# Attention maxima from three of six bf16 products on two halves of the array's rows, with PSUM evictions moved to ScalarE and numerators copied out early

## The chip, the cores and the metric

The kernel runs on one core of one Trainium2 chip. The metric is the device time of one execution in microseconds (us), the median over runs. Engines are named as in the profile: PE (TensorE matmul), PEld (its weight loads), DVE (VectorE), ACT (ScalarE), POOL (GpSimd), SP (SyncE, which here only issues DMAs).

## The reference, cut to what matters

The program is one layer of three parts on an input of 2 x 1024 x 512: a differential attention with a low-pass filter over time, a second attention-like block, and a mixture of experts. The change lies in the first part:

```
q, k = rope(x @ Wq), rope(x @ Wk)            # 16 heads, each with two streams w of D = 16
s[w] = q[w] @ k[w].T * D**-0.5, causal mask  # T = 1024 queries and keys
a[w] = softmax(s[w]);  o[w] = a[w] @ v       # v has 2*D = 32 columns per head
y    = lowpass(o[0] - lambda * o[1])         # rfft, times a Gaussian, irfft along T
y    = y * rsqrt(mean(y*y over 32) + eps) * w_rms * (1 - LAMBDA_INIT);  out = y @ Wout
```

## The kernel before, in words

The function `attention` handles 8 groups g (2 batches x 4 groups of 4 heads), each with two streams: 16 "sets" n = 2g + w. In float32 the scores would need slow matmuls, so q and k are each cut into three bf16 pieces (16 rows each) and six products of pieces are summed by stacking them along the contraction: `qst` and `kst` hold 6 x 16 = 96 rows for each of the 4 heads, and two more rows (96, 97) that carry the softmax shift as two bf16 pieces against ones.

For each set the kernel does two passes over the scores. The **rows** pass (L703 to 718) computes scores with queries on the partitions, 96 rows deep, and DVE takes minus their maximum along the keys (L839, `maxima`). The maxima of a half of the queries are cut into two bf16 pieces on DVE (`shift_pieces`, L820 to 823), turned by PE into a row (`shifts`, L696), copied by DVE (L830), and brought by two DMAs on SP's queue (`shift_in`, L586 to 590) into rows 96 and 97 of `qst`. The **probs** pass (L720 to 733) computes the scores again with keys on the partitions, 98 rows deep, so that they come out with the shift subtracted; ACT takes their exp into `prob` (L951). Each four heads of one block of keys then make one **values** step (L735 to 749): float32 matmuls of the probabilities with v into `acc` and with ones into `den`, four heads side by side on 32 output columns each ("128*32" in the profile). When a half of the queries is done, ACT makes 1/den (`norm`, L939 and L941) and DVE multiplies and adds into `oT` (`output`, L847, or L851 and L854). The next half's first values step waits for `s_den` and `s_acc`.

All of PE's score units share five PSUM banks (RING = 5): a unit waits in `slot_free` until the unit five before it was read. One PSUM bank, `misc`, serves everything else in turn: the projections of group g + 2 (`project`, in sets with odd n), and in sets with even n the chain of group g - 1: `turn` (transposes), `low` (the filter, six parts), `square` (mean of squares). DVE reads `misc` in all of these (L786, L800, L801, L807, L812, L830), and POOL applies the rotation and cuts the pieces (`rotate`, L966 to 975, seven operations, then a DMA of the pieces) and does the squares and the last scaling (L988, L994 to 998).

The order of the work is a list made by `schedule`: units of set n's probs are merged evenly with those of set n + 1's rows (48 and 38, so 86 to a set), and every other step is put behind a unit by a fixed count. Every engine walks that one list in order. SP's queue has an order of its own (L626 to 645): in each set it issues `stack(n + 2)` (12 DMAs), `shift_in(n + 1, 0)`, for even n `store(g - 1)`, which waits for POOL's last scaling, in the last but one set also `weights_ahead` (11 DMAs of the next part's weights), and then `shift_in(n + 1, 1)`.

## Time and profile before

| | us |
|---|---|
| median of 3 runs (lowest to highest) | 1603.81 (1602.01 to 1616.31) |
| the profiled execution, its own time | 1599.38 |
| its span, first to last instruction | 1597.8 |
| PE matmul busy / DVE / ACT / POOL busy in the span | 1326.1 / 946.8 / 511.7 / 569.5 |
| mean granted clock of TensorE | 0.925 of 2.4 GHz |

The program runs three stages: normalisation up to 71 us, attention from 74 to about 1093 us, the rest behind that. Busy time of PE overlaps between neighbouring matmuls, since their ends are modelled, so spacings from start to start are what one costs in a stream.

### The profile page before, as it was taken

Reading aid. Unit: us, or ns where it says so; the run is one execution under the profiler, and the core shown is the slowest. Engines: PE = TensorE matmul, PEld = TensorE weight load, DVE = VectorE, ACT = ScalarE, POOL = GpSimd, SP = SyncE. Lnnn points to the kernel's source line nnn. Section 1 sums busy time; section 2 is a strip of 40 time slices with the busy share of each in tenths; the row PEclk is TensorE's granted clock in tenths of the full one; section 3 lists DMA queues with packets and bytes.
Section 4 is the critical chain, followed back from the end, with each engine's and each line's share of the span. In section 5 each row is a group of like instructions: output and inputs, shape, how many; then the busy total and the mean of one; then the engine's idle time right before and its main releaser. Section 6 shows DMA issues by size and latency. Waiting matters only on the chain. (4 is left out here: it accounts for less than half of the span.)

```text
span 1597.8 us, 23263 instructions
## 1 busy us (share of the span) xinstructions
PE 1326.1 (83%) x8077; PEld 683.6 (43%) x8092; DVE 946.8 (59%) x1774; ACT 511.7 (32%) x1149; POOL 569.5 (36%) x655
## 2 busy tenths in 40 slices
PE   6867989989989989989989999875688978875985
PEld 5623334434433434433433434332566655552542
DVE  6558666556565566565565566317577655542886
ACT  2200533533433433433433454533112111110121
POOL 4425133333333333333333300200277666663211
PEclk9988999999989999989999999987799998997998
DMA  4345332232231231221331230302222221012331
GB/s 147 120 118 90 74 61 60 42 60 61 41 61 53 49 57 57 48 43 54 53 55 51 43 55 2 120 1 94 78 68 67 67 66 62 36 47 79 123 102 40
DMA packets 70713, 103.92 MB, mean 65 GB/s; under 512 B 10064, under 2 KB 36048, under 8 KB 70608
## 3 DMA queue, kind: packets, MB, share of 16 engines
q1 hardware_dynamic: 58832, 69.00, 19.7%
q0 software_dynamic: 7168, 25.17, 4.5%
q10 hardware_dynamic: 4608, 8.39, 1.4%
q8 instruction: 61, 1.00, 0.3%
q14 instruction: 44, 0.36, 0.1%
HBM read 68.72 MB, written 33.82 MB: 64 GB/s over the span
## 5 line engine op out<-in xcount | busy, mean ns | idle before, releaser
L839 DVE TENSOR_REDUCE nm<-score 128x1 f32<-128x512 f32 (+3 forms) x608 | 379.0, 658 | 287.1 <-PE score L716 156.9
L951 ACT ACTIVATE prob<-score 128x512 f32<-128x512 f32 (+3 forms) x768 | 347.7, 490 | 530.4 <-PE score L731 340.5
L727 PE MATMUL score<-qst,kst 98*128 98x512 bf16 (+3 forms) x768 | 250.5, 342 | 9.1 <-DVE nm L839 4.0
L711 PE MATMUL score<-kst,qst 96*128 96x512 bf16 (+3 forms) x768 | 232.2, 341 | 10.4 <-DMA kst<-piece_scratch 5.4
L746 PE MATMUL acc<-prob,vg 128*32 128x512 f32 (+3 forms) x1536 | 173.9, 526 | 41.9 <-DVE second L851 20.9
L746 PE MATMUL den<-prob,ones 128*32 128x512 f32 (+3 forms) x1536 | 169.8, 514 | 0.0
L660 PE MATMUL misc<-xnT,wg 128*128 128x512 f32 x256 | 137.8, 638 | 21.8 <-DVE raw L786 14.8
L966 POOL TENSOR_TENSOR rot<-raw,cos 128x1024 f32<-128x1024 f32 x14 | 32.8, 2341 | 328.4 <-DVE swapped L792 328.4
L727 PEld LDWEIGHTS score<-qst,kst 98*128 98x128 bf16 x768 | 75.9, 99 | 143.8 <-issue 88.8
L711 PEld LDWEIGHTS score<-kst,qst 96*128 96x128 bf16 x768 | 71.9, 102 | 119.6 <-issue 70.3
L731 PE MATMUL score<-mask_t,identb 128*128 128x128 bf16 x512 | 111.2, 223 | 0.0
L988 POOL TENSOR_TENSOR sq<-y 128x512 f32<-128x512 f32 x14 | 14.5, 1036 | 230.4 <-DVE y L807 161.9
L716 PE MATMUL score<-mask_s,identb 128*128 128x128 bf16 (+2 forms) x352 | 89.2, 254 | 0.0
L746 PEld LDWEIGHTS den<-prob,ones 128*32 128x32 f32 x1536 | 53.5, 116 | 80.9 <-issue 75.1
L1291 PE MATMUL m_b<-m_winh,m_hTh 128*128 128x512 f32 x192 | 85.8, 447 | 2.5 <-DVE m_hTl L1423 2.5
L1291 PE MATMUL m_b<-m_winh,m_hTl 128*128 128x512 f32 x192 | 77.7, 404 | 0.0
L1291 PE MATMUL m_b<-m_winl,m_hTh 128*128 128x512 f32 x192 | 77.0, 401 | 0.0
L746 PEld LDWEIGHTS acc<-prob,vg 128*32 128x32 f32 x1536 | 31.9, 110 | 100.2 <-ACT prob L951 79.6
L660 PEld LDWEIGHTS misc<-xnT,wg 128*128 128x128 f32 x256 | 45.2, 202 | 53.5 <-issue 40.4
L1678 PE MATMUL l_z<-xnT,l_qT 128*128 128x512 f32 x128 | 59.3, 609 | 7.9 <-DMA l_res<-res_scratch 7.9
L731 PEld LDWEIGHTS score<-mask_t,identb 128*128 128x128 bf16 x512 | 51.0, 100 | 29.1 <-issue 16.1
L786 DVE TENSOR_SCALAR raw<-misc 128x512 f32<-128x512 f32 x32 | 22.1, 692 | 67.5 <-PE misc L660 67.4
(227 smaller groups left out, 2140.3 us busy)
## 6 DMA issues: line engine op xcount, KB each, us to landing
piece_scratch<-pieces POOLq DMA_DIRECT2D x16, 768.0 KB, 4.7
qst<-piece_scratch SPq DMA_DIRECT2D x96, 128.0 KB, 5.5
kst<-piece_scratch SPq DMA_DIRECT2D x96, 128.0 KB, 7.5
x1in<-in_query SPq DMA_DIRECT2D x16, 256.0 KB, 2.7
v_scratch<-v ACTq DMA_DIRECT2D x16, 256.0 KB, 2.0
vg<-v_scratch SPq DMA_DIRECT2D x8, 512.0 KB, 6.3
att_scratch<-y SPq DMA_DIRECT2D x8, 512.0 KB, 2.6
m_aT<-att_scratch SPq DMA_DIRECT2D x16, 256.0 KB, 2.9
```

Of the source, the lines that this page charges most:

```text
L660: mm = nc.tensor.matmul(misc[:], wg[:, g % 2, c, w], xnT[:, c, base:base + HALF], start=(c == 0), stop=(c == KC - 1))
L711: mm = nc.tensor.matmul(bank[:, x], qst[0:PROD, n % 4, first + x, i * P:(i + 1) * P], kst[0:PROD, n % 4, first + x, c0:c0 + width], start= ...
L716: mm = nc.tensor.matmul(bank[:, :, width - P:width], identb[:], mask, start=False, stop=True, skip_group_check=True)
L727: mm = nc.tensor.matmul(bank[:, t0:HALF], kst[0:ROWS, n % 4, head, j * P:(j + 1) * P], qst[0:ROWS, n % 4, head, h * HALF + t0:(h + 1) * HA ...
L731: mm = nc.tensor.matmul(bank[:, t0:t0 + P], identb[:], mask_t[:], start=False, stop=True, skip_group_check=True)
L746: mm = nc.tensor.matmul(bank[x, t0:HALF], ones[:] if total else vg[:, n // 2 % 2, j, x], prob[:, (n * NPU + v * GH + head) % NPROB, t0:HAL ...
L786: nc.vector.tensor_scalar(raw[:, half(h)], misc[:], (1.0, float(D) ** -0.5)[w], None, ALU.mult)\
L839: nc.vector.tensor_reduce(dst[:, first:first + heads].rearrange("p (a o) -> p a o", o=1), score[k % RING][:, 0:heads * width].rearrange("p ...
L951: nc.scalar.activation(prob[:, p % NPROB, t0:HALF], score[k % RING][:, t0:HALF], ACT.Exp)\
L966: nc.gpsimd.tensor_tensor(rot[:], raw[:], cos[:], ALU.mult).then_inc(s_cosm, 1)
L1291: mm = mmul(b[:], x[:, c * P:(c + 1) * P], y[:, c, col:col + E], start=(c == 0 and n == 0), stop=(c == KC - 1 and n == 2))
L1678: mm = nc.tensor.matmul(z[t.c % 2][:], qT[:, t.slot, c], rhs, start=(c == 0), stop=(c == KC - 1))
```

## The change

The stacked rows of even and odd heads get different layouts. Even heads have their bands at partitions 0, 16, ... 80 and the shift at 96 and 97, as before; odd heads have them at 64, 80, 96, 16, 32, 48, the shift at 0 and 1, and zeros in rows 2 to 15. The order of pieces is such that the first three bands hold the products 0x0, 1x0 and 0x1. The rows pass now uses these 48 rows alone: partitions 0 to 47 for an even head, 64 to 111 for an odd one. A rows unit is of heads of one parity, units come in pairs (even, odd) whose matmuls alternate and write two banks; there are 40 units to a set where there were 38. The probs pass uses all six products as before (98 rows for even heads, 112 for odd). The list is now merged in pairs (24 + 20 to a set) and all distances are counted in pairs. The steps that share `misc` are kept three pairs apart. ACT instead of DVE copies out `misc` for projections, turns and the filter; DVE keeps the swap, the squares and the shift row. At the end of a half ACT copies `acc` into `accs` in SBUF, on which PE's next values step now waits, and DVE multiplies and adds from that copy. `stack` issues 24 DMAs of half the size, the shift is read back by two DMAs, and POOL sets constants by four memsets, behind the first pieces instead of ahead of them.

```diff
-PROD = 6 * D
-ROWS = PROD + 2
+BANDS = ((0, 16, 32, 48, 64, 80), (64, 80, 96, 16, 32, 48))
+PIECE = ((0, 1, 0, 2, 1, 0), (0, 0, 1, 0, 1, 2))
+COARSE = (slice(0, 3 * D), slice(64, 64 + 3 * D))
+SHIFT = (slice(6 * D, 6 * D + 2), slice(0, 2))
+FULL = (slice(0, 6 * D + 2), slice(0, 64 + 3 * D))
 def rows_units():
     units = []
     for i in range(TB):
         for c0 in range(0, (i + 1) * P, HALF):
             width = min(HALF, (i + 1) * P - c0)
-            n = max(1, HALF // width) if width != 384 else 1
-            units += [(i, c0, width, h, n) for h in range(0, GH, n)]
+            n = 2 if width <= HALF // 2 else 1
+            for first in range(0, 2, n):
+                for odd in range(2):
+                    units.append((i, c0, width, [2 * x + odd for x in range(first, first + n)]))
...
-VALUES_LATER, NORM_LATER, OUT_LATER, SUMS_LATER = 4, 3, 6, 5
+VALUES_LATER, NORM_LATER, OUT_LATER, SUMS_LATER, MISC_FREE = 3, 1, 4, 6, 3
...
+    pairs += [("rows", 0, u) for u in range(0, NRU, 2)]
...
+        mine = [("probs", n, m) for m in range(0, NPU, 2)]
+        ahead = [("rows", n + 1, u) for u in range(0, NRU, 2)] if n + 1 < SETS else []
+        pairs += merge(mine, ahead)
...
+        for h, last in enumerate((at["rows", n, FIRST_HALF - 2], at["rows", n, NRU - 2])):
+            put(last + 1, ("sums", n, h))
+            use(last + SUMS_LATER, ("shift", n, h))
...
-            k = at["probs", n, v * GH + GH - 1] + VALUES_LATER
+            k = at["probs", n, v * GH + GH - 2] + VALUES_LATER
...
-        if n % 2 == 0 and g > 0 or n == SETS:
-            for k, name in zip((14, 17, 27, 41, 46, 54), ("turn", "turn", "low", "low", "square", "square")):
-                use(s + k, (name, g - 1, int(k in (17, 41, 54))))
-            put(s + 50, ("root", g - 1, 0))
-            put(s + 58, ("root", g - 1, 1))
+        s = start[n]
+        if n % 2 == 0 and g > 0:
+            for k, name in zip((8, 10, 17, 23, 27, 30), ("turn", "turn", "low", "low", "square", "square")):
+                use(s + k, (name, g - 1, int(k in (10, 23, 30))))
         if n % 2 and g + 2 < B * G:
-            for k, w, h in ((14, 0, 0), (22, 0, 1), (56, 1, 0), (66, 1, 1)):
+            for k, w, h in ((8, 0, 0), (15, 0, 1), (29, 1, 0), (35, 1, 1)):
                 use(s + k, ("proj", g + 2, w, h))
+    free = 0
+    for first, _, name in sorted(wanted):
+        k = max(first, free)
+        last = PARTS.get(name[0], 1) - 1
+        for part in range(last):
+            put(k + part, ("part", name, part))
+        put(k + last, ("use", name, last))
+        if name[0] == "square":
+            put(k + 2, ("root", *name[1:]))
+        free = k + last + MISC_FREE
...
+                    for odd in range(2):
+                        for r, piece in zip(BANDS[odd], PIECE[w]):
+                            src = piece_scr[g % 2, w, piece].rearrange("(b p w d) t -> w p d b t", p=2, w=2, d=D)
+                            sp.dma_start(parity((qst, kst)[w][r:r + D], odd)[:, slot], src[n % 2, odd])\
+                                .then_inc(s_stack[slot], 16)
...
-                sp.dma_start(qst[PROD:ROWS, n % 4, :, half(h)], shift_scr[n % 2, h]).then_inc(s_shdma[h], 16)
+                for odd in range(2):
+                    sp.dma_start(parity(qst[SHIFT[odd]], odd)[:, n % 4, :, half(h)],
+                                 shift_scr[n % 2, h].rearrange("s (b p) t -> p s b t", p=2)[odd])\
+                        .then_inc(s_shdma[h], 16)
...
+                banks = []
+                for odd in range(2):
+                    slot_free(k + odd)
+                    heads = RU[u + odd][3]
+                    banks.append(score[(k + odd) % RING][:, 0:len(heads) * width]
+                                 .rearrange("p (a s) -> p a s", a=len(heads)))
+                diag = c0 + width == (i + 1) * P
+                for x in range(len(heads)):
+                    for odd in range(2):
+                        c, head = COARSE[odd], RU[u + odd][3][x]
+                        mm = nc.tensor.matmul(banks[odd][:, x], qst[c, n % 4, head, i * P:(i + 1) * P],
+                                              kst[c, n % 4, head, c0:c0 + width], start=(x == 0),
+                                              stop=(x == len(heads) - 1), skip_group_check=True)
+                        if x == len(heads) - 1 and not diag:
+                            mm.then_inc(s_unit, 1)
+                if diag:
+                    mask = mask_s[:].rearrange("p (o s) -> p o s", o=1).broadcast_to([P, len(heads), P])
+                    for odd in range(2):
+                        nc.tensor.matmul(banks[odd][:, :, width - P:width], identb[:], mask, start=False, stop=True,
+                                         skip_group_check=True).then_inc(s_unit, 1)
...
-                    pe.wait_ge(s_acc, 2 * n + h)
+                    pe.wait_ge(s_accs, 2 * n + h)
...
+            def swap(g, w):
+                r = 2 * g + w
+                dve.wait_ge(s_mread, order["proj", g, w, 1])
...
                 if n % 2 == 0:
-                    nc.vector.tensor_tensor(oT[:, half(h)], acc[:], rden[:, q % 2], ALU.mult).then_inc(s_acc, 1)
+                    if g > 0:
+                        dve.wait_ge(s_misc, order["turn", g - 1, h])
+                    nc.vector.tensor_tensor(oT[:, half(h)], accs[:, q % 2], rden[:, q % 2], ALU.mult)\
+                        .then_inc(s_mul, 1)
                 else:
-                    if n > 1 or h:
-                        dve.wait_ge(s_oT, 2 * g + h)
-                    nc.vector.scalar_tensor_tensor(second[:], acc[:], nlam[:], rden[:, q % 2], ALU.mult, ALU.mult)\
-                        .then_inc(s_acc, 1)
-                    dve.wait_ge(s_acc, q + 1)
-                    nc.vector.tensor_tensor(oT[:, half(h)], oT[:, half(h)], second[:], ALU.add).then_inc(s_oT, 1)
+                    nc.vector.scalar_tensor_tensor(accs[:, q % 2], accs[:, q % 2], nlam[:], rden[:, q % 2],
+                                                   ALU.mult, ALU.mult).then_inc(s_mul, 1)
+                    dve.wait_ge(s_mul, q + 1)
+                    nc.vector.tensor_tensor(oT[:, half(h)], oT[:, half(h)], accs[:, q % 2], ALU.add).then_inc(s_oT, 1)
...
+            def project(g, w, h):
+                number, r = order["proj", g, w, h], 2 * g + w
+                act.wait_ge(s_misc, number)
+                if r >= 1:
+                    act.wait_ge(s_cosm, r)
+                nc.scalar.mul(raw[:, half(h)], misc[:], (1.0, float(D) ** -0.5)[w]).then_inc(s_mread, 1)
+            def turned(g, h):
+                act.wait_ge(s_misc, order["turn", g, h])
+                src = misc[:].rearrange("p (j c) -> p j c", j=4)
+                nc.scalar.copy(onat[:, 4 * h:4 * h + 4], src).then_inc(s_nat, 1)
+                nc.scalar.copy(onb[:, 4 * h:4 * h + 4], src).then_inc(s_nat, 1)
+                act.wait_ge(s_nat, 4 * g + 2 * h + 2)
+                act.sem_inc(s_mread, 1)
+            def filtered(g, h):
+                act.wait_ge(s_misc, order["low", g, h])
+                if g >= 1:
+                    act.wait_ge(s_attdma, 16 * g)
+                nc.scalar.copy(y[:, half(h)], misc[:]).then_inc(s_mread, 1)
...
-                if q >= 2:
-                    act.wait_ge(s_acc, q - 1)
+                if n % 2:
+                    act.wait_ge(s_mul, q - 1)
+                elif n > 0:
+                    act.wait_ge(s_oT, n - 1 + h)
                 nc.scalar.activation(rden[:, q % 2], den[:], ACT.Ln).then_inc(s_den, 1)
+                nc.scalar.copy(accs[:, q % 2], acc[:]).then_inc(s_accs, 1)
                 act.wait_ge(s_den, q + 1)
+                act.wait_ge(s_accs, q + 1)
                 nc.scalar.activation(rden[:, q % 2], rden[:, q % 2], ACT.Exp, scale=-1.0).then_inc(s_rden, 1)
...
-            nc.gpsimd.memset(ones[:], 1.0).then_inc(s_ones, 1)
-            pool.wait_ge(s_ones, 1)
-            nc.gpsimd.memset(kst[PROD:P], 1.0).then_inc(s_ones, 1)
-            pool.wait_ge(s_ones, 2)
             for w in range(2):
                 pool.wait_ge(s_rot, 6 * (w + 1))
                 pieces_out(0, w)
+            nc.gpsimd.memset(ones[:], 1.0).then_inc(s_ones, 1)
+            pool.wait_ge(s_ones, 1)
+            nc.gpsimd.memset(parity(kst[SHIFT[0]], 0), 1.0).then_inc(s_ones, 1)
+            pool.wait_ge(s_ones, 2)
+            nc.gpsimd.memset(parity(qst[0:D], 1), 0.0).then_inc(s_ones, 1)
+            pool.wait_ge(s_ones, 3)
+            nc.gpsimd.memset(parity(kst[0:D], 1), 0.0).then_inc(s_ones, 1)
+            pool.wait_ge(s_ones, 4)
+            nc.gpsimd.memset(parity(kst[SHIFT[1]], 1), 1.0).then_inc(s_ones, 1)
+            pool.wait_ge(s_ones, 5)
             pool.wait_ge(s_const, 16 * 12)
```

## Rows read from the trace of the kernel before

**Rows 1.** Busy time by engine, attention and one group of two sets (columns: stretch, length, busy and count of PE, PEld, DVE, ACT, POOL, then clock, DMA share, GB/s).

```profile
150.00:1060.00 910.00, 813.24 (x6062) 352.36 (x6080) 527.76 (x840) 395.03 (x858) 275.89 (x188) 0.95 0.26 53
461.80:582.30 120.50, 107.65 (x782) 47.04 (x784) 72.85 (x113) 50.27 (x108) 41.22 (x29) 0.94 0.26 54
464.00:470.90 6.90, 4.90 (x31) 2.21 (x32) 4.81 (x7) 2.10 (x4) 6.68 (x4) 0.51 0.01 4
```

**Rows 2.** What PE waited for in the same group (us in total, times, longest).

```profile
PE misc L696 <- DVE shp L823: 5.7, 2, 3.9
PE acc L746 <- DVE second L851: 2.5, 2, 1.4
```

**Rows 3.** PE in order of time, 501.1 to 502.8 us (start, duration in us).

```profile
501.23 0.22 PE L731 MATMUL score<-mask_t,identb 128*128 128x128 bf16 x1
501.38 0.64 PE L746 MATMUL acc<-prob,vg 128*32 128x256 f32 x8
501.83 0.61 PE L746 MATMUL den<-prob,ones 128*32 128x256 f32 x8
502.38 0.23 PE L727 MATMUL score<-qst,kst 98*128 98x128 bf16 x1
502.45 0.22 PE L731 MATMUL score<-mask_t,identb 128*128 128x128 bf16 x1
502.51 0.38 PE L711 MATMUL score<-kst,qst 96*128 96x512 bf16 x1
502.73 0.22 PE L716 MATMUL score<-mask_s,identb 128*128 128x128 bf16 x1
```

**Rows 4.** Groups of instructions by line and shape (count, busy us, mean ns, idle before).

```profile
L839 DVE TENSOR_REDUCE nm<-score 128x1 f32<-128x512 f32 x384 | 251.2, 686 | 162.3 <-PE score L711 121.5 <-PE score L716 35.0 <-DVE y L807 0.2
L345 ACT COPY v<-n_vp 128x512 f32<-128x512 f32 x16 | 9.4, 588 | 27.2 <-PE n_vp L325 27.2
```

**Rows 5.** DVE, POOL and PE in order of time, 461 to 466.1 us.

```profile
461.19 2.34 POOL L966 TENSOR_TENSOR rot<-raw,cos 128x1024 f32<-128x1024 f32 x1 [27.29 <-DVE swapped L792]
...
463.49 2.34 POOL L967 TENSOR_TENSOR swapped<-swapped,sin 128x1024 f32<-128x1024 f32 x1
463.59 2.26 DVE L823 TENSOR_TENSOR shp<-nm,shp 128x16 bf16<-128x16 f32 x1
...
466.00 0.37 PE L696 MATMUL misc<-identb,shp 128*8 128x128 bf16 x2 [3.87 <-DVE shp L823]
```

**Rows 6.** DVE and POOL in order of time, 472 to 473.8 us.

```profile
472.05 0.74 DVE L851 SCALAR_TENSOR_TENSOR second<-acc,nlam,rden 128x512 f32<-128x512 f32 x1
472.73 2.13 POOL L975 TENSOR_TENSOR pieces<-rot,pieces 128x1024 bf16<-128x1024 f32 x1
472.83 2.58 DVE L854 TENSOR_TENSOR oT<-oT,second 128x512 f32<-128x512 f32 x1
```

**Rows 7.** The start of attention in order of time.

```profile
74.45 13.75 POOL L1003 MEMSET kst<- 32x16384 bf16 x1
...
98.01 0.69 DVE L786 TENSOR_SCALAR raw<-misc 128x512 f32<-128x512 f32 x1
...
98.84 5.38 PE L660 MATMUL misc<-xnT,wg 128*128 128x512 f32 x8 [6.10 <-DVE raw L786]
...
118.26 2.65 SPq L584 DMA_DIRECT2D kst<-piece_scratch  x6
```

**Rows 8.** POOL's scaling of one group in order of time, first and last of ten operations.

```profile
664.37 1.04 POOL L994 TENSOR_TENSOR newton<-rs 128x512 f32<-128x512 f32 x1 [5.26 <-ACT rs L932]
...
674.88 1.27 POOL L998 TENSOR_TENSOR y<-y,newton 128x512 f32<-128x512 f32 x1
```

**Rows 9.** SP's queue in order of time, 1016 to 1033 us.

```profile
1016.10 0.38 SPq L594 DMA_DIRECT2D att_scratch<-y  x1
...
1025.73 1.89 SPq L588 DMA_DIRECT2D shift_scratch<-shrow  x1
...
1032.35 0.61 SPq L590 DMA_DIRECT2D qst<-shift_scratch  x1
```

**Rows 10.** PE at 1034.55 us, in order of time.

```profile
1034.55 1.89 PE L727 MATMUL score<-qst,kst 98*128 98x512 bf16 x4 [3.40 <-DMA qst<-shift_scratch]
```

More of the change, by code:

```diff
@@ L413, in schedule @@
 def schedule():
-    units, start = [], []
-    units += [("rows", 0, u) for u in range(NRU)]
+    pairs, start = [], []
+    pairs += [("rows", 0, u) for u in range(0, NRU, 2)]
     for n in range(SETS):
-        start.append(len(units))
-        mine = [("probs", n, m) for m in range(NPU)]
-        ahead = [("rows", n + 1, u) for u in range(NRU)] if n + 1 < SETS else []
-        units += merge(mine, ahead)
-    start.append(len(units))
-    at = {u: k for k, u in enumerate(units)}
+        start.append(len(pairs))
+        mine = [("probs", n, m) for m in range(0, NPU, 2)]
+        ahead = [("rows", n + 1, u) for u in range(0, NRU, 2)] if n + 1 < SETS else []
+        pairs += merge(mine, ahead)
+    start.append(len(pairs))
+    at = {u: k for k, u in enumerate(pairs)}
     behind = {}
@@ L427, in put, with use @@
         behind.setdefault(k, []).append(event)
-    def use(k, name, spread=1):
-        last = PARTS.get(name[0], 1) - 1
-        for part in range(last):
-            put(k - (last - part) * spread, ("part", name, part))
-        put(k, ("use", name, last))
+    wanted = []
+    def use(k, name):
+        wanted.append((k - PARTS.get(name[0], 1) + 1, len(wanted), name))
     before = [("use", ("proj", 0, w, h), KC - 1) for w in range(2) for h in range(2)]
@@ L518, in attention @@
         rden = sb("rden", [P, 2, HALF])
-        second = sb("second", [P, HALF])
+        accs = sb("accs", [P, 2, HALF])
         oT = sb("oT", [P, T])
@@ L705, in rows @@
             def rows(n, u):
-                i, c0, width, first, heads = RU[u]
                 k = place["rows", n, u]
-                slot_free(k)
-                bank = score[k % RING][:, 0:heads * width].rearrange("p (a s) -> p a s", a=heads)
-                for x in range(heads):
-                    mm = nc.tensor.matmul(bank[:, x], qst[0:PROD, n % 4, first + x, i * P:(i + 1) * P],
-                                          kst[0:PROD, n % 4, first + x, c0:c0 + width], start=(x == 0),
-                                          stop=(x == heads - 1), skip_group_check=True)
@@ L755, in _ @@
                             pe.wait_ge(s_const, 16 * 12)
[L756 removed]
+                        pe.wait_ge(s_stack[x % 4], 384 * (x // 4 + 1))
                     rows(x, u)
@@ L834, in maxima @@
             def maxima(n, u):
-                i, c0, width, first, heads = RU[u]
+                i, c0, width, heads = RU[u]
                 k = place["rows", n, u]
@@ L880, in _ @@
                         nc.vector.tensor_reduce(lam_e[:], lam_p[:], AX.X, ALU.add).then_inc(s_lam, 1)
+                        begun = 1
+                    maxima(x, u)
+                    maxima(x, u + 1)
+                elif kind == "sums":
+                    shift_pieces(x, u)
+                elif kind == "out":
+                    if (x, u) == (0, 0):
                         dve.wait_ge(s_lam, 4)
@@ L956, in _ @@
                     root(x, u)
-            for h in range(2):
-                root(NG - 1, h)
+                elif kind == "use":
+                    if x[0] == "proj":
+                        project(*x[1:])
+                    elif x[0] == "turn":
+                        turned(*x[1:])
+                    elif x[0] == "low":
+                        filtered(*x[1:])
+            g = NG - 1
+            for h in range(2):
+                turned(g, h)
+            for h in range(2):
+                filtered(g, h)
+            for h in range(2):
+                root(g, h)
         @block.gpsimd
```

145 lines of the change are left out of this document (57 added, 88 removed).

## The prediction

> **What bounds the kernel now.** I read the busy table over stretches first, because the share of the whole span mixes three stages. In attention (150 to 1060 us) PE has matmuls in 813 of 910 us; DVE is busy 58%, ACT 43%, POOL 30% [rows 1]. The stage repeats with a period of two sets, one group: 461.8 to 582.3 is one, 120.5 us, and there are 7.5 of them with two kinds of work merged (15 sets). In it PE idles 12.9 us (120.5 less 107.65), and its granted clock is 0.94. The 6% missing are stretches at the lower level of 1.2 GHz, as 464.0 to 470.9 at 0.51, and they start while PE stands: they cost 0.06 x 120.5 = 7.2 us. That leaves 120.5 - 12.9 - 7.2 = 100.4 us of PE work at full clock.
>
> The waits of PE in this group then say who holds it up: DVE's shift pieces 5.7 and `second` 2.5 [rows 2]; nearly all the rest are DVE too. Why is DVE late when it idles 40% of the time? In order of time L823, a subtraction of 16 numbers, takes 2.26 us while POOL's rotation is in L967, and PE gets its pieces 3.87 us late [rows 5]. At 472.8 L854 (oT + second, both in SBUF) takes 2.58 us beside POOL's L975, but L851, which reads `acc` from PSUM, takes its 0.74 although POOL starts L975 inside it [rows 6]. So a DVE operation with two inputs in SBUF waits until the POOL operation under way ends; one that reads a score or `acc` from PSUM doesn't.
>
> **Part 1, half of the rows matmuls beside the other half.** A set has 18,432 columns of rows matmuls, a group 36,864, or 72 times 512. One of 512 takes 0.22 us from start to start [rows 3]: 15.8 us. If even and odd run side by side, 7.9 go. Taking 48 instead of 96 rows gains nothing by itself: what is paid is columns.
>
> But PE now changes the shape of its array. The trace has this for columns: from the mask (0.06 us for 128 columns, 502.45 to 502.51) to `acc` takes 0.15, so 0.09 extra; `acc` to `den` is 0.45, `den` to the next probs 0.55, so 0.10 extra [rows 3]. One change is 0.095 us. I counted changes along the list of events: 56 in a group before (values and shift rows, in and out), 121 after (36 + 5 into the two halves and 35 + 4 out of them, the rest as before, with some values steps straight beside a rows pair). 65 x 0.095 = 6.2 us come back. No row shows a change of row shape. Its bounds are nothing (6.2 us less) and 0.19, twice the column one (6.2 more, if the second half's weights must also be loaded in the open). I take 0.095, the only change that the trace shows. Sum of part 1: -1.7 us a group. That the two halves overlap at all no row shows either; the four column strips of a values step do: four heads of `acc`, each of 256 columns in float32, take 0.45 us together [rows 3]. I take full overlap; the bound is none, +7.9.
>
> The Trainium skill (TensorEngine Tiling (Array Packing), Key Properties) says that a change of tiling mode "drains the TensorE", and that different tiles run in parallel. The 0.095 us above agree for columns; whether it holds for rows, no run here shows yet. By that page alone the part would be near nothing, as I have it.
>
> DVE has 40 maxima operations in place of 38 with the same elements; two more of 256 columns are well under 2 x 0.69 us [rows 4], beside PE work. The mask matmuls stay (4,096 columns a set).
>
> **Part 2, evictions on ACT, `acc` copied early.** ACT gets 4 projections, 4 turn copies, 2 filter copies and 4 copies of `acc` in a group, 14 x 0.59 = 8.3 us [rows 4]; it goes from 50.3 to 58.6 of about 116 us, beside other work. DVE loses 10 x 0.69. `second` (2.5 us of PE's waiting) goes as a wait; next late is ACT: at a set's end the next values step comes only three probs pairs and a rows pair later, and ln and copy (0.59 each by the copy's row) stand behind two exps. I put 0.5 us a group there, the rest under the stalls of DVE.
>
> **Part 3, POOL against DVE, which speaks against the change.** `output` now reads `accs` and `rden`, two inputs in SBUF, where it read PSUM: the operation that was immune in [rows 6] is so no more. And the steps moved against POOL. A rotation takes 13.7 us (461.19 to 474.86) [rows 5, 6]. I laid the events out with the durations above; times are from a set's start:
> - Odd set, first rotation: before, it began at `sums(n + 1, 0)`, which is why L823 was late. Now the sums are at pair 14, ahead of the projection (pair 18): that wait goes. But `out(n, 0)` at pair 21 falls into the first two POOL operations. It has 1.0 and up to 2.3 us to wait; DVE comes back 3 to 3.5 us late, and five banks cover about one rows pair. PE stands 4.4 us.
> - Even set, second rotation: its projection ends at pair 36 of 44, so POOL works from 3 us ahead of the set to 10 us into it. `sums(n, 1)` waits 2.3 us, `out` 1 to 2: PE stands 3.1 us, about as before.
> - Start of an odd set: POOL's scaling takes 11.8 us [rows 8]. `root(g - 1, 1)` stood behind unit 58 of 86 (67% of the set), now behind pair 39 of 44 (89%), so the scaling reaches 7 us into the next set and delays its sums: 1.6 us.
> - A rows pair needs two banks at once. Between values steps DVE takes 2 x 0.69 for a pair and PE 1.0 for a rows and a probs pair (three times 0.22, 0.19 for the changes, masks): about 0.25 us at 12 of 24 values steps, 3 us.
>
> Together 12.1 + 0.5 = 12.6 us against 12.9. The clock follows long stalls; with one of 4.4 and one of 3.1 in place of more and closer ones I take 5 us for 7.2. Bounds of stalls and clock together: 6 us (DVE is idle often enough that only the 4.4 us remain) and 29 (each collision meets the full 2.3 us).
>
> The skill's page SBUF — State Buffer, Who interferes with whom, has it that a DVE instruction with two SBUF inputs contends with a GpSimd instruction that reads SBUF. The trace agrees in L854 (2.58 us).
>
> A group: -1.7 - 0.3 - 2.2 = -4.2; times 7.5: **-32 us**.
>
> **Part 4, start and end.** In the first group DVE's copy of `misc` stood behind the whole rotation, until 98.01, and PE idled 6.10 us for it [rows 7]. ACT can copy inside that rotation. Then the copy, the next matmuls and their copy (0.69 + 5.38 + 0.69) are done before DVE is free, and its second rotation starts 6.8 us sooner. The rows wait for six more DMA issues of `kst` at 2.65 / 6 = 0.44 us each [rows 7], 2.6: **about -4.5 us** (bounds 0 and -7). The memsets move behind the first pieces and take about twice 13.75 us [rows 7], since each still covers half the columns; POOL's rotation of group 1 moves to about 136 us, with a set to spare. At no cost: DVE is the bound of the first rows pass (38 x 0.69 = 26 us of maxima) and PE's wait there is hidden.
>
> At the end there is a loss. `store(6)` on SP waits for the last scaling but one; behind it stand 11 weight DMAs and then `shift_in(15, 1)`. The store went out at 1016.10, the shift at 1025.73 and came back at 1032.35 [rows 9], and PE waited 3.40 us [rows 10]. The scaling is now later by 89 - 67 = 22% of a 50 us set, 11 us; set 15 has no other work for PE: **+10 us**. In the other sets the same delay stays under the 16 us until the shift is needed.
>
> **Sum.** 1599.4 - 32 - 4.5 + 10 = 1573. The profiled execution is 4.4 us under the median of the runs, so the forecast is **1577 us**, -1.7%.
>
> **The rivals.**
> - The change of row shape is free. For it: weights of each row half may load while the other rows compute; against: the column change costs 0.095. Then 7.5 x 6.2 = 46 us less: 1531. Chance 0.20.
> - The stalls nearly vanish. For it: the wait on L823 and that on `second`, 8.2 of 12.9 us, are undone as such, and DVE loses 6.9 us of work. Against: the POOL rows. Stalls 6 and clock 2 instead of 17.6: 7.5 x -9.6 = -72: 1505. Chance 0.13.
> - The halves take turns on the array: +7.9 x 7.5 = 59: 1636, slower. The change then doesn't do what it says. Chance 0.10.
> - The other side by one mechanism: DVE's operations with two SBUF inputs meet POOL in full. Six to eight such operations a group each wait 2.3 us, PE stalls 20 us and not 12.6: +7.5 x 7.4 = 56, 1633. It decides as soon as DVE is held longer than the five banks cover, about 1.4 us. Chance 0.13.
> - My forecast, 1550 to 1600: chance 0.44, of which 0.32 below 1588.
>
> **From cases to numbers.** 1% is 16 us, about what a measurement of this kernel can tell. Faster by more: 0.32 + 0.20 + 0.13 = 0.65, less 0.05 for what I haven't thought of: 0.60. Within 1%: 0.12 and 0.05 of the slower cases: 0.17. Slower: 0.23. The range takes in the free switch, the vanished stalls and both slower cases: 1505 to 1640.
>
> **What the profile will show.** Rows matmuls as "48*128" in pairs a few ns apart, the pair of 512 done in about 0.22 us (part 1), and a gap of 0.1 us ahead of it and behind it. `accs` operations of DVE with a maximum over 2 us (part 3). PE's waits on `second` gone, waits on nm L839's successor in their place. The last shift's wait over 10 us. A period of about 116 us. Wrong if the gap around row pairs is nil or 0.2, or if DVE never waits for POOL.

## The result and the profile after

The changed kernel takes 1619.75 us (median; 1617.43 to 1625.60), the kernel before, in the same rounds, 1604.11: a ratio of 1.009, 95% interval 1.0068 to 1.0113. It is slower by 0.9%, where 1577 us, 1.7% faster, was forecast; it lies inside the range of 1505 to 1640 us, on the side away from the forecast. The profiled execution has a span of 1618.9 us at a mean clock of 0.912, against 1597.8 at 0.925.

Where the 21 us of span come from I read from one mark, the first exp of each set (every 48th of ACT's 768 probs exps in order of time):

| stretch | before | after | difference | forecast |
|---|---|---|---|---|
| start to set 0 | 154.3 | 157.8 | +3.5 | -4.5 |
| set 0 to set 15 | 866.2 | 875.6 | +9.4 | -32 |
| set 15 to its last exp | 38.9 | 46.8 | +7.9 | +10 |
| rest | 538.4 | 538.7 | +0.3 | 0 |

One group after, and inside it the 6.8 us behind its longest stall (columns as in [rows 1]):

```profile
387.62:510.43 122.81, 108.98 (x789) 42.31 (x789) 65.05 (x106) 55.19 (x122) 42.12 (x29) 0.93 0.20 53
478.30:485.10 6.80, 6.52 (x29) 1.66 (x30) 2.49 (x5) 1.21 (x3) 6.51 (x5) 0.54 0.01 2
```

PE idles 122.81 - 108.98 = 13.8 us (12.9 before), although DVE has 7.8 us less of work (65.05 us and not 72.85 [rows 1]). What it waits for in this group:

```profile
PE score L738 <- DVE nm L850: 9.6, 9, 4.6
PE score L756 <- ACT prob L989: 2.2, 2, 1.5
PE score L756 <- DVE nm L850: 1.6, 1, 1.6
```

The waits on the shift pieces and on `second` [rows 2] are gone, and waits on maxima have their place. The largest, in order of time on POOL, DVE and PE:

```profile
471.61 2.36 POOL L1024 TENSOR_TENSOR rot<-raw,cos 128x1024 f32<-128x1024 f32 x1 [21.25 <-DVE swapped L816]
472.01 2.51 DVE L864 SCALAR_TENSOR_TENSOR accs<-accs,nlam,rden 128x512 f32<-128x512 f32 x1
473.93 2.79 POOL L1025 TENSOR_TENSOR swapped<-swapped,sin 128x1024 f32<-128x1024 f32 x1
474.55 2.71 DVE L867 TENSOR_TENSOR oT<-oT,accs 128x512 f32<-128x512 f32 x1
...
478.58 0.61 PE L738 MATMUL score<-kst,qst 48*128 48x512 bf16 x2 [4.60 <-DVE nm L850]
```

L864 is the step that took 0.74 from PSUM in [rows 6]; from `accs` it takes 2.51. The two steps hold DVE 5.2 us, no maxima run, PE stands 4.60 us, and the clock falls at that moment: 0.54 over the next 6.8 us, the level of 1.2 GHz, in the window above. Two more waits have no term in the prediction, each once per group:

```profile
438.58 1.04 POOL L1052 TENSOR_TENSOR newton<-rs 128x512 f32<-128x512 f32 x1 [9.24 <-ACT rs L967]
...
441.76 1.28 POOL L1055 TENSOR_TENSOR newton<-newton,rs 128x512 f32<-128x512 f32 x1
443.13 0.63 ACT L965 ACTIVATE rs<-sq 128x512 f32<-128x512 f32 x1 [3.53 <-POOL newton L1055]
...
444.64 0.23 PE L756 MATMUL score<-qst,kst 112*128 112x128 bf16 x1 [1.49 <-ACT prob L989]
...
501.49 1.07 PE L680 MATMUL misc<-xnT,wg 128*128 128x512 f32 x2
502.60 0.60 ACT L945 ACTIVATE raw<-misc 128x512 f32<-128x512 f32 x1 [0.27 <-PE misc L680]
503.24 0.01 DVE L816 LOAD_MASK_SELECT swapped<-raw  x1 [3.94 <-ACT raw L945]
...
505.15 0.28 PE L756 MATMUL score<-qst,kst 112*128 112x256 bf16 x1 [1.65 <-DVE nm L850]
```

First, ACT's second root (L965) uses the same `rs` as the first, so it waits 3.53 us for POOL's scaling, with the exps behind it in ACT's order. Second, DVE reaches the swap in its written order and stands 3.94 us, from 499.30. ACT is the last link of that wait and not the long one: its copy took 0.60 us and began 0.04 us after the projection's last matmul had ended (501.49 + 1.07 = 502.56). So 3.3 of the 3.94 us are a wait for PE. Both waits were there before, shorter:

```profile
494.69 0.69 DVE L786 TENSOR_SCALAR raw<-misc 128x512 f32<-128x512 f32 x1 [1.49 <-PE misc L660]
...
548.89 0.63 ACT L930 ACTIVATE rs<-sq 128x512 f32<-128x512 f32 x1 [1.35 <-POOL newton L997]
```

The one for the root cost PE 0.23 us then and 1.49 now. What lengthened them is not shown by a run; the list merged in pairs, with other distances between projection, swap and roots, is the likely cause, since the runs below shorten them by distances alone.

The start, POOL, ACT and PE:

```profile
108.05 6.92 POOL L1064 MEMSET kst<- 2x8192 bf16 x1
...
128.97 6.92 POOL L1070 MEMSET kst<- 2x8192 bf16 x1
135.97 2.33 POOL L1024 TENSOR_TENSOR rot<-raw,cos 128x1024 f32<-128x1024 f32 x1
138.40 0.60 ACT L945 ACTIVATE raw<-misc 128x512 f32<-128x512 f32 x1 [31.86 <-POOL rot L1024]
139.14 2.05 PE L680 MATMUL misc<-xnT,wg 128*128 128x512 f32 x2 [6.66 <-ACT raw L945]
157.10 0.58 PE L756 MATMUL score<-qst,kst 98*128 98x512 bf16 x1 [5.07 <-DMA qst<-shift_scratch]
```

And the end, SP's queue and PE:

```profile
1038.05 0.38 SPq L614 DMA_DIRECT2D att_scratch<-y  x1
1038.47 2.59 SPq L637 DMA_DIRECT2D xnT<-in_W_in  x4
...
1047.82 0.77 SPq L605 DMA_DIRECT2D shift_scratch<-shrow  x1
1053.68 1.24 SPq L608 DMA_DIRECT2D qst<-shift_scratch  x2
1056.20 1.03 PE L756 MATMUL score<-qst,kst 98*128 98x512 bf16 x2 [13.40 <-DMA qst<-shift_scratch]
```

### The profile page after: what moved, and what is told of

Read it like the earlier page. It is cut to its first block and busy times, and to the rows that moved or that the text cites. A ratio compares the mean times of both kernels' runs of the same rounds, so it can differ in the third digit from the quotient of the medians.

```text
span 1618.9 us, 23935 instructions
## 1 busy us (share of the span) xinstructions
PE 1328.0 (82%) x8109; PEld 646.1 (40%) x8124; DVE 893.4 (55%) x1726; ACT 553.4 (34%) x1261; POOL 587.2 (36%) x658
## 5 line engine op out<-in xcount | busy, mean ns | idle before, releaser
L989 ACT ACTIVATE prob<-score 128x512 f32<-128x512 f32 (+3 forms) x768 | 328.9, 489 | 414.6 <-PE score L760 286.6
L756 PE MATMUL score<-qst,kst 98*128 98x512 bf16 (+7 forms) x768 | 221.0, 350 | 44.7 <-DMA qst<-shift_scratch 18.5
L738 PE MATMUL score<-kst,qst 48*128 48x512 bf16 (+3 forms) x768 | 125.3, 350 | 80.9 <-DVE nm L850 67.9
L680 PE MATMUL misc<-xnT,wg 128*128 128x512 f32 x256 | 139.9, 640 | 17.6 <-ACT raw L945 10.6
L756 PEld LDWEIGHTS score<-qst,kst 98*128 98x128 bf16 (+1 forms) x768 | 74.9, 103 | 178.1 <-issue 62.8
L738 PEld LDWEIGHTS score<-kst,qst 48*128 48x128 bf16 x768 | 34.7, 95 | 202.6 <-issue 132.1
L760 PE MATMUL score<-mask_t,identb 128*128 128x128 bf16 x512 | 109.0, 230 | 0.0
L746 PE MATMUL score<-mask_s,identb 128*128 128x128 bf16 (+1 forms) x384 | 66.4, 257 | 0.0
L1355 PEld LDWEIGHTS m_b<-m_winh,m_hTh 128*128 128x128 f32 x192 | 37.6, 196 | 33.4 <-issue 21.2
```

The source lines that it names most:

```text
L680: mm = nc.tensor.matmul(misc[:], wg[:, g % 2, c, w], xnT[:, c, base:base + HALF], start=(c == 0), stop=(c == KC - 1))
L738: mm = nc.tensor.matmul(banks[odd][:, x], qst[c, n % 4, head, i * P:(i + 1) * P], kst[c, n % 4, head, c0:c0 + width], start=(x == 0), stop ...
L746: nc.tensor.matmul(banks[odd][:, :, width - P:width], identb[:], mask, start=False, stop=True, skip_group_check=True).then_inc(s_unit, 1)
L756: mm = nc.tensor.matmul(bank[:, t0:HALF], kst[c, n % 4, head, j * P:(j + 1) * P], qst[c, n % 4, head, h * HALF + t0:(h + 1) * HALF], start ...
L760: mm = nc.tensor.matmul(bank[:, t0:t0 + P], identb[:], mask_t[:], start=False, stop=True, skip_group_check=True)
L989: nc.scalar.activation(prob[:, p % NPROB, t0:HALF], score[k % RING][:, t0:HALF], ACT.Exp)\
```

## The experiments

All in one table. "Sets" is the time from set 0 to set 15, "period" the mean of the five groups from set 3 to set 13, "half rate" how much of a period PE's granted clock is 0.5, from the clock's stretches in the trace, "idle" one group's length less PE's busy time. The last four columns are of one profiled execution each. The ratio is to the kernel before in the same rounds; its median was 1602.2 to 1607.3 us there, so a difference of two medians from different rounds is good to about 3 us. I count half of the half-rate time as what the clock costs. That is somewhat too much: PE is busy 103.0 us per period at full clock throughout (pool_short_before, below) and 108.0 before with 13.7 us at half rate, so 5.0 and not 6.9; and 102.0 in a group of comb_keys against 109.0 after, so 7.0 and not 8.6.

| kernel | us, median | ratio to before (95%) | sets | period | half rate | idle |
|---|---|---|---|---|---|---|
| before | 1604.11 | 1 | 866.2 | 120.9 | 13.7 | 12.9 |
| after | 1619.75 | 1.009 (1.007 to 1.011) | 875.6 | 122.8 | 17.1 | 13.8 |
| swap_late | 1566.39 | 0.974 (0.970 to 0.979) | 821.8 | 113.8 | 7.2 | 8.9 |
| swap_w0 | 1580.80 | 0.985 (0.979 to 0.990) | 835.2 | 116.0 | 10.2 | 9.6 |
| pool_short_after | 1558.79 | 0.970 (0.965 to 0.974) | 816.1 | 112.6 | 5.9 | 8.2 |
| pool_short_before | 1548.14 | 0.963 (0.958 to 0.969) | 806.3 | 111.1 | 0 | 8.1 |
| root_late | 1598.63 | 0.997 (0.994 to 1.000) | 847.3 | 118.4 | 8.2 | 13.0 |
| num_psum | 1627.30 | 1.014 (1.005 to 1.022) | 876.2 | 121.6 | 11.4 | 14.6 |
| memset_order | 1614.11 | 1.004 (1.001 to 1.007) | 872.9 | - | - | - |
| tail_order | 1609.50 | 1.002 (0.999 to 1.006) | 876.2 | - | - | - |
| same_half | 1663.98 | 1.027 (1.014 to 1.040), of the two shorter of its four runs | 925.6 | 129.2 | 23.2 | 10.6 (8.9 in every other group) |
| six_products | 1611.06 | 1.003 (1.000 to 1.007) | 875.0 | 122.9 | 17.1 | 13.0 |
| combined | 1542.87 | 0.961 (0.957 to 0.965) | 812.7 | 112.6 | 6.8 | 7.8 |
| comb_six | 1543.32 | 0.960 (0.956 to 0.965) | 813.7 | 112.7 | 6.8 | 7.3 |
| comb_keys | 1528.25 | 0.951 (0.947 to 0.956) | 796.1 | 109.8 | 2.0 | 6.9 |
| comb_six_keys | 1523.39 | 0.948 (0.943 to 0.954) | 794.0 | 109.3 | 0 | 6.4 |

**When the rotation starts: swap_late, swap_w0.** The swap becomes an event of its own (for queries, keys), so that POOL starts later:

```diff
         put(k + last, ("use", name, last))
+        if name[0] == "proj" and name[3] == 1:
+            put(k + last + (4, 2)[name[2]], ("swap", name[1], name[2]))
```

> The changed kernel, with DVE's pair swap placed four pairs behind the projection for queries (so behind the first-half output of the odd set) and two pairs behind the one for keys, from group 2 on. My theory (POOL's rotation, started by the swap, stretches DVE's two-SBUF-input output from 1.5 to 5.2 us and PE then waits 4.6 us; and DVE stands 3.9 us at the swap, in its list order, for ACT's copy of the projection, for which PE waits 1.65 + 0.53 us): both stalls go in the 6 groups that have a rotation, 6.8 x 6 = -41 us less what comes next in line, so -20 to -40 us, about 1587. Rival (PE's stalls only move, since the ring is bound by DVE's work as a whole and the clock gives back what is gained): within 5 us of 1620. Rival (the key rotation, now 2.7 us later, meets the second-half output): 0 to -20.

swap_w0 has (4, 0) in place of (4, 2).

> The changed kernel with the swap for queries alone placed behind the first-half output (four pairs), that for keys left where it is. Theory, by parts: this takes the 4.6 us stall (output under POOL) and what the clock adds, and leaves the wait of DVE for ACT at the key swap (1.65 + 0.53 us): -6 us per group, about 1582, that is two thirds to three quarters of the 53 us that both moves gave. Rival (the key swap's wait for ACT was the dearer one): above 1600.

With both, 53 us go, more than the 20 to 40 expected; with the queries' swap alone, 39, as expected. The queries' swap takes 6.8 us off the period: the 4.60 us stall (idle 4.2 less in all) and 6.9 us less of half rate, which by the half had cost 3.4. The keys' swap takes 2.2 more. PE's 1.65 us behind it are 0.17, but PE's two waits under the rotation that it starts have grown from 2.28 and 0.47 to 2.54 and 1.00, so idle falls by 0.7 only; the rest is the clock's. "The stalls only move" is refuted. One group of swap_late:

```profile
429.00:542.90 113.90, 105.00 (x789) 41.59 (x788) 63.45 (x107) 55.06 (x122) 41.62 (x29) 0.97 0.21 57
```

POOL is as busy as before; it works at another time.

**Without most of POOL's rotation: pool_short_after, pool_short_before.** The seven operations of `rotate` on `[:, 0:P]` instead of `[:]`, in either kernel, so that the other 896 columns are left out.

> The changed kernel, with the seven POOL operations of each rotation (from group 1 on) on 128 of the 1024 columns, so that the rest of queries and keys isn't rotated; all else as it is. If POOL's hold on DVE's two-SBUF-input operations is what ate the gain, the 4.6 us and 2.3 us stalls of each group go and the time falls by 6.9 x 7 = 48 us at most, about -25 to -45. What would stay: the wait of DVE for ACT at the swap (1.65 + 0.53) and the 1.5 us of ACT behind POOL's normalisation. Rival (POOL is no cause, the maxima themselves are): within 8 us of 1620.

> The kernel before with the same cut of POOL's rotations. Before, DVE's output reads PSUM and does not meet POOL (0.74 us always); only the sums and the add do. My theory: the gain here is smaller than in the changed kernel, -5 to -25 us, so that the changed kernel without rotation is the faster of the two. Rival (the rotation cost both the same, the loss is in the schedule of pairs or in ACT): equal gains in both.

One group each, after and then before, so cut:

```profile
424.90:537.50 112.60, 104.42 (x789) 41.26 (x788) 59.05 (x108) 54.95 (x123) 21.51 (x29) 0.98 0.21 58
```

```profile
420.50:531.60 111.10, 103.00 (x787) 45.84 (x785) 64.97 (x114) 50.15 (x108) 20.23 (x28) 1.00 0.30 58
```

Here my theory fell. The cut is worth 10.2 us of a period in the changed kernel and 9.8 in the one before. POOL's rotation cost both the same, so it isn't by a greater cost of POOL that the change lost; it lost by gaining nothing there, and without the rotation it is still slower by 1.5 us per period (1558.8 against 1548.1, though the runs of the second spread from 1539 to 1559). The rival that the rest lies in schedule and ACT stands: PE's waits of 1.66 us behind the swap and 1.49 behind the root are in the cut kernel as well, and two half-rate stretches in this group, while before, so cut, has none in its profiled execution.

**ACT behind POOL: root_late.** `put(k + (2, 5)[name[2]], ("root", ...))` for `put(k + 2, ...)`: the second half's root three pairs later.

> The changed kernel with the second half's root on ACT put three pairs later, so that ACT no longer stands up to 3.5 us for POOL's normalisation with the numerators of the next units behind it. Theory: PE's 1.49 us wait once per group goes, 7 x 1.5 = 10 us, and up to as much again if the half-rate stretch of 3.4 us that follows it goes too: -8 to -20 us, about 1608. Rival (the ring has slack there and another wait takes its place): within 4 us of 1620.

21 us, just over the upper end of 20. PE's wait is 0.55 instead of 1.49, and idle falls by 0.8 us only; the half-rate time falls from 17.1 to 8.2, which by the half, 4.4, is as much as the whole gain per period. Taking this one wait away also spared part of the clock loss at other stalls. Why it reached those, the runs don't show.

**The early copy: num_psum.** No copy of `acc` by ACT; DVE's output reads PSUM and PE's next numerators wait for it.

> The changed kernel with ACT's early copy of the numerators taken out: DVE's output reads them from PSUM, as before, and PE's next numerators wait for it. My theory (the copy moved the output's first step into the class of operations with two inputs in SBUF, which POOL holds up): that step is 0.75 us again under POOL's rotation instead of 1.2 to 2.5, PE's 4.6 us stall falls to about 3, and PE gets a wait of about 1.7 us behind the output four times per group: between -10 and +25 us in all, likeliest +10, about 1630. Rival (the early copy costs and saves nothing): within 5 us of 1620.

```profile
595.98 0.75 DVE L863 SCALAR_TENSOR_TENSOR accs<-acc,nlam,rden 128x512 f32<-128x512 f32 x1
596.76 1.72 DVE L866 TENSOR_TENSOR oT<-oT,accs 128x512 f32<-128x512 f32 x1
```

```profile
596.88 1.60 PE L775 MATMUL acc<-prob,vg 128*32 128x512 f32 x8 [2.43 <-DVE accs L863]
```

POOL's L1021 ran from 595.59, and the PSUM-reading step took 0.75 inside it: confirmed. PE then waited 2.43 us for that step instead of 4.60 for maxima, and 1.43 more behind another output. From set 0 to set 15 the two are equal (876.2 and 875.6); by the medians num_psum is 7.5 us longer, with intervals and runs that overlap. So from set 0 to set 15 the early copy gave and cost about nothing; whether it gave some us elsewhere stays open.

**The halves of the array: same_half, six_products, comb_six, comb_six_keys.** `BANDS`, `SHIFT` and `FULL` of odd heads set to those of even ones, `COARSE` to `slice(0, 3 * D)` for both (same_half) or `slice(0, 6 * D)` (six_products, and the same on the combined kernels). In all of them the two memsets of zeros become short ones on 512 columns.

> The changed kernel with odd heads stacked like even ones: both heads of a pair read rows 0 to 47 of the array (the other 16-row bands at 48 to 97), so that the two take turns; the same instructions and the same switches between rows. The two 6.92 us memsets of zeros go with it, so the start is shorter by some 6 us; what counts is the time from the first numerators of set 0 to those of set 15 (875.6 us in the changed kernel). If the overlap of halves is worth what the trace shows (starts 3 ns apart; 107 us of columns fewer in all), the row matmuls are longer by 7.9 us per group on PE, of which part goes into PE's idle time of 13.8 per group: +20 to +55 us on that stretch. Rival (the stretch is bound by DVE and its stalls, the overlap buys only idle time): +0 to +10 us.

> The changed kernel with the maxima from all six products (rows 0 to 95 for both heads, the same stacking, no halves and nearly no change of row shape) and pairs, copies and schedule as changed; without the two memsets of zeros. By the measured terms the halves are worth 7.9 us per group on PE less 6.2 for the changes of shape: within 5 us of the changed kernel's 875.6 us from set 0 to set 15, +1.7 x 7.5 = +13 at most. Since both heads of a pair taking turns without that saving cost +44 us in all, a rival: it is the serial columns that cost, and six products are as dear as that, +35 us or more. Another: the changes of shape cost more than columns (they start the half-rate stretches), and six products are faster, by 10 us or more.

> The combined kernel (1542.87 us, 812.7 from set 0 to set 15) with the maxima from six products for both heads (no halves, no change of row shape but at masks and numerators, no memsets of zeros). In the changed kernel this exchange left the groups as they were (875.0 against 875.6), which could be since the stalls bounded them. Theory A (halves and changes of shape cancel wherever PE is the bound: -7.9 + 6.2 per group): six products slower by 1.7 x 7.5 = 13 us on that stretch. Theory B (the stretch is held by the ring, where a pair is released as a whole and the overlap only ends it earlier): within 4 us. Theory C (with stalls gone the changes of shape are what is left between this and 111.1 us per group): six products faster by 5 us or more.

The same pair of 512 columns behind a projection and ahead of probs, in the changed kernel, same_half and six_products:

```profile
501.97 0.59 PE L680 MATMUL misc<-xnT,wg 128*128 128x512 f32 x1
502.50 0.39 PE L738 MATMUL score<-kst,qst 48*128 48x512 bf16 x2
502.82 0.28 PE L756 MATMUL score<-qst,kst 98*128 98x256 bf16 x1
```

```profile
521.36 0.59 PE L680 MATMUL misc<-xnT,wg 128*128 128x512 f32 x1
521.88 0.60 PE L738 MATMUL score<-kst,qst 48*128 48x512 bf16 x2
522.42 0.28 PE L756 MATMUL score<-qst,kst 98*128 98x256 bf16 x1
```

```profile
491.81 0.60 PE L738 MATMUL score<-kst,qst 96*128 96x512 bf16 x2
492.25 0.27 PE L756 MATMUL score<-qst,kst 98*128 98x256 bf16 x1
```

From the pair to the probs: 0.32 with the halves together, 0.54 taking turns, 0.44 in one shape. So 0.22 is the overlap and 0.10 the change of row shape, and there is one more such change ahead of the pair. Per group, PE's work at full clock is length less idle less clock: 122.8 - 13.8 - 8.6 = 100.4 in the changed kernel, 132.1 - 10.6 - 0.10 x 132.1 = 108.3 in same_half, 122.9 - 13.0 - 8.6 = 101.3 in six_products. Halves are worth 7.9, changes of shape 7.0: net -0.9, and the time from set 0 to 15 moves by 0.6 us. (The 8.7 us between the medians of six_products and the changed kernel lie ahead of set 0, which begins at 148.7 instead of 157.8 without the long memsets.) same_half's four runs spread from 1640 to 1671 us, and the profiled one, 1670.61, is the longest, so I take the terms from it and not its total; with the clock's share as uncertain as said above they are good to about 1 us. The rows just shown, all at full clock, give the overlap by themselves: 0.22 x 36 pairs = 7.9.

On the combined kernel six products give 813.7 against 812.7, and 1543.32 against 1542.87; with earlier keys 794.0 against 796.1. The halves and their changes cancel with the stalls and without: that is the range of theory B, within 4 us, and it ran against my guess that they were only hidden. In one group of each, PE is busy 104.84 us in combined and 105.55 in comb_six, and idles 7.8 and 7.2: the 0.7 us that the halves save come back as idle time. That fits theory B; that it is the ring that takes them back is argued and not shown. The medians of comb_six and comb_six_keys also hold a start that is 2.9 and 2.5 us shorter without the long memsets.

**Start and end: memset_order, tail_order.** Three memsets ahead of `pieces_out(0, 0)`, the fourth between the two pieces; and for the last set `shift_in(n + 1, 1)` ahead of `store` and `weights_ahead`.

> The changed kernel with three of POOL's four 6.92 us memsets ahead of the first pieces (POOL is idle from 68.5 to 98.1 us there) and the fourth between the two pieces' DMA issues. Theory: POOL's first rotation starts at about 108 instead of 136 us, ACT's copy of the projection no longer waits for it (31.9 us), PE's waits of 6.7 and 5.1 us in the start go: -8 to -12 us, about 1609. Rival (the shift rows' trip through memory is late for another reason, DVE's row pass of the start is the bound): PE's wait at the first numerators stays and the gain is under 3 us.

> The changed kernel with the last set's second transfer of the shift rows issued by SP ahead of the store of group 6 and of the ten loads of later weights. Theory: the transfer is issued some 10 us earlier, PE's wait of 13.4 us at 1056 falls to about 2 to 3: -9 to -12 us, about 1609. Rival (the transfer waits for the rows themselves, DVE's copy, not for SP's list; or the loads share the queues with it): under 3 us. A second rival (the later weights land late and the next stage pays): the gain at 1056 is given back behind 1080.

tail_order: PE's 13.40 us became 2.93, the median 10.3 less, as expected. memset_order: the long wait of ACT went (the copy follows its matmul at once), set 0 began 4.5 us sooner, at 153.3, but the median fell by 5.6 and not by 8 to 12 (by the ratios of the two it is 8.8, so it may have reached the lower end): the shift rows' wait stayed at 4.24 us, and the memsets now held DVE (last section).

**Together: combined, comb_keys.** Combined is the two late swaps, the late root, the memsets and the tail. comb_keys then has the projection for keys at (24, 29) instead of (29, 35) and its swap one pair behind.

> The changed kernel with the four moves that paid each alone: swaps later (1566.4), second root later (1598.6), memsets ahead of the first pieces (1614.1) and the last shift rows ahead of store and weights (1609.5), against 1619.75. If the stalls are separate and add up: 53 + 21 + 6 + 10 = 90 us less, about 1530. If the gains of the two in the groups overlap (both include the clock's share of the same stretches), 1535 to 1550. Rival (another wait takes over at once): no better than 1560.

> The combined kernel with the projection for keys five to six pairs earlier and its swap one pair behind it, so that the rotation of keys (14.4 us on POOL) ends about when the sums of the next set begin. Theory (the last long stall, 2.53 us behind sums that took 2.27 us under POOL, and the 6.8 us at half rate that begins right then, are the rotation's meeting with the sums): 2.5 + 3.4 us per group less, six groups, -25 to -35 us, about 1512. Rival (the sums still meet the rotation's last steps, or the queries' rotation meets the earlier projection's copy): 0 to -10.

> Both together: earlier keys and six products. If what the halves do depends on whether stalls bound the stretch, the difference to the kernel with earlier keys alone is larger here than that of the other pair of this call: by theory A +13 us from set 0 to set 15, by theory B within 4, by theory C -5 or more.

Combined: 1542.87, in the range for overlapping gains; one stretch of 6.8 us at half rate is left per group. comb_keys: 14.6 less, half of what I expected. The stall behind the sums fell from 2.5 to about 1.6 only, since their last step still meets the rotation's end, but of the half-rate stretch of 6.8 us behind it, which combined has in six groups, three are gone and two are half as long. One group of comb_keys and one of comb_six_keys:

```profile
416.30:525.20 108.90, 101.96 (x787) 40.63 (x790) 62.04 (x107) 54.53 (x124) 41.41 (x29) 1.00 0.22 60
```

```profile
413.80:523.10 109.30, 102.95 (x787) 46.12 (x789) 61.73 (x107) 54.52 (x124) 41.43 (x29) 1.00 0.22 59
```

At full clock the difference in PE's work is seen without any correction: 102.95 - 101.96 = 1.0 us in favour of the halves, of which 0.6 are idle time again. The best version is comb_six_keys at 1523.39, 0.948 of before; against comb_keys its runs overlap and its start is shorter by the memsets, so which of the two is faster stays open. Either is 6% under the changed kernel with nothing but times of issue altered (and, in the first, six products again).

## Why the prediction was wrong, step by step

**Part 1 was right.** Rows matmuls start a few ns apart (322 ns from the pair to the probs), a change costs 0.10, the overlap 7.9 per group as forecast, the changes 7.0 for 6.2, net -0.9 for -1.7. Full overlap and 0.095 were the right choices between their ends. The Trainium skill (TensorEngine Tiling (Array Packing), Key Properties) has it that a change of tiling mode drains TensorE and that tiles run in parallel. The rows agree for halves of the rows too: a gap of 0.10 us at a change, and pairs that start 3 ns apart.

**Part 2: the copies fit, the waits had no term.** The copies fit into ACT's time, 55.19 us as against 58.6 forecast. But I put only 0.5 us for waits there, at a set's end, and never asked where, in the new list, DVE meets the swap and ACT the second root. DVE stood at the swap for the projection (1.65 us of PE's time), and PE behind ACT's exps behind the root (1.49 us): 3.1 us. (The 0.53 us that I counted with the swap are in swap_late as well, 0.54.) The moved copy is not the cause of the first: 3.3 of DVE's 3.94 us were PE's matmuls, and my expectation for swap_late, that DVE stands there for ACT's copy, says too much. swap_w0 against swap_late (2.2 us per period) and root_late show that both places were costly.

**Part 3, the stalls: right in kind, near in sum.** Output under POOL: 4.4 forecast, 4.60 measured. Sums under the second rotation: 2.28 of the 3.1 for that spot. Start of the odd set: 1.6, measured 0.27 + 0.47. Another 3.0 in waits of 0.2 to 0.7 us stand beside the 3 us that I gave the pairs. The sum was 12.6, measured 13.8: what I had terms for came to about 10.7, and the two waits above are the rest. One reading was incomplete: in [rows 5] it was not L823 alone that was late. The cast ahead of it, also on 16 numbers, took 1.91 us until POOL's operation ended, and takes 0.17 when none is under way as it begins:

```profile
461.64 1.91 DVE L822 CAST shp<-nm 128x16 bf16<-128x16 f32 x1
```

So POOL's arithmetic holds a cast of DVE, with one input, as well as an operation with two. That the contention costs this change more than the kernel before, which I had as a rival and first believed after the result, is refuted by the pair of cut kernels.

**The clock term was the step that failed most.** "With one of 4.4 and one of 3.1 in place of more and closer ones I take 5 us for 7.2" had no row under it. The half-rate time per period rose from 13.7 to 17.1 us, by the half from 6.9 to 8.6: in five groups 15 low stretches and not 12. So the term was +1.7 where -2.2 was forecast, 3.9 us per group; the stalls were +0.9 for -0.3, 1.2; PE's work -0.7 for -1.7, 1.0. Together that is the 6.1 by which the group was missed (+1.9 instead of -4.2); with the clock priced from the kernels at full clock it is 4.2, 1.2 and 0.7. The whole stretch missed by 41 us, -32 and +9.4. Why the low level came more often no run shows; swap_late, root_late and the combined kernels show only that it goes as single stalls do.

**Part 4, start: "at no cost" failed.** The rows did begin sooner, at 118.84 us, but I priced POOL's memsets for DVE and PE's rows and forgot what POOL's first rotation releases: ACT's next copy of `misc`, for which PE's projection, the shift and then set 0 wait. -4.5 became +3.5. In memset_order set 0 began 4.5 us sooner, so 4.5 of the 8 came back. **End: right**, 13.40 us of waiting, +7.9 for +10, and tail_order shows the cause as named.

The rival of POOL "in full" (1633) came nearer in time than the forecast, but not by its mechanism: its 20 us of stalls weren't there. That it lies nearer is luck.

## What to carry to other kernels

Moving work to an idle engine doesn't free the engines that read its result in a written order: look for who is next in that order, follow the wait past the last link to the one that is long (here PE's matmuls behind ACT's copy), and put the reader as many steps later as that needs. Where the clock falls behind single stalls, a stall costs itself and nearly half the low stretch behind it, and where it goes is worth trying by moving one event, since here four moves of issue time were worth 77 us and the whole change of the arithmetic nothing. A saving on one engine that needs changes of array shape has to be counted in changes: 65 of about 0.1 us ate 7.0 of the 7.9 us of columns.

## What the hardware showed that I had not expected

In memset_order DVE's own rotation ran beside POOL's memset. DVE's L876 to L879, two float32 inputs in SBUF, took their usual 1.23 us under it, but the cast behind them didn't:

```profile
100.37 6.91 POOL L1069 MEMSET kst<- 2x8192 bf16 x1
```

```profile
102.50 1.23 DVE L879 TENSOR_TENSOR rot<-rot,swapped 128x1024 f32<-128x1024 f32 x1
103.76 4.07 DVE L880 CAST pieces<-rot 128x1024 bf16<-128x1024 f32 x1
...
109.13 0.69 DVE L882 CAST pieces<-rot 128x1024 bf16<-128x1024 f32 x1
```

The cast, 0.69 us alone, ended 0.55 us after the memset did; the first rotation's cast took 2.20 in the same way. So a memset, which only writes, lets two inputs pass and holds up the cast, where POOL's arithmetic held both (2.51 us on L864, 1.91 us on the cast L822 before). The Trainium skill has both (SBUF — State Buffer, Who interferes with whom): two SBUF inputs contend with a GpSimd instruction that reads SBUF, "not with one that only writes it", while casts can run in a mode that holds the shared ports. These rows agree with it.

A memset of 8192 bf16 per partition took 6.92 us on 2 partitions and on 16: narrowing it in partitions saves nothing.
